# Four spectral layers on one core: tensors between layers stored by unit, image, column and row

## The chip, the cores and the metric

The kernel runs on one NeuronCore of a Trainium2 chip. The metric is the device time of one execution in microseconds (us), the median of several. The engines that are named below are TensorE (PE; its weight loads are a row of their own, PEld), VectorE (DVE), ScalarE (ACT), GpSimd (POOL), and SyncE (SP). SP computes nothing here: it issues every transfer of the kernel, on one queue, and waits in order for what each transfer needs.

## The reference

The input is `x` of shape (2, 64, 64, 384) in float32: two images, 64 rows, 64 columns, 384 channels. Four layers follow each other. Each is a two-dimensional Fourier mixer with a two-step product per block of 48 channels, and adds its input at the end:

```python
xs = jnp.fft.rfft2(xf32, axes=(1, 2)).reshape(B, H, Wm, NUM_HEADS, BLOCK)
o1r = jax.nn.relu(einsum(xr, w1[0]) - einsum(xi, w1[1]) + b1[0])   # and o1i
o2r = einsum(o1r, w2[0]) - einsum(o1i, w2[1]) + b2[0]              # and o2i
out = jnp.fft.irfft2(softshrink(o2r, LAMBDA) + 1j * softshrink(o2i, LAMBDA), s=(H, W), axes=(1, 2))
return out + x
```

Layer 1 differs: it normalises each pixel over its channels first, uses a GELU and no shrinking, keeps half of the row frequencies, and is followed by a token MLP:

```python
h = afno2d(_ln(x, ln1_g, ln1_b), w1, b1, w2, b2) + x
m = _ln(h, ln2_g, ln2_b)
return _gelu(m @ mlp_w1 + mlp_b1) @ mlp_w2 + mlp_b2 + h            # 384 -> 1536 -> 384
```

## The kernel before

The 384 channels are cut into 8 blocks of 48, and two blocks make a **unit** (96 channels, `PAIR`). So each layer has 4 units (`PAIRS`), and the four layers have 16, numbered 0 to 15; units 4 to 7 are layer 1. A unit lies in one of three SBUF buffers `xs` of 128 partitions x 64 rows x 96 channels (3072 KB): the partition is (image, column), so 64 partitions hold one image. It is loaded whole, worked on in place (the residual sum is written into it), and stored.

**The spectral part** runs over blocks `g`. POOL (in layer 1: ACT and DVE) makes `xn` from `xs`. PE then does `f1` (the transform over rows, `xn` as weights), `f2` (over columns), `m1` and `m2` (the two products), `f5` and `f6` (the inverse transforms). Except in `m1` and `f6` its matmuls are short, 32 to 96 columns, with a weight load before each. ACT and DVE move results out of PSUM between these steps; DVE's `f6` adds the last one to `xs` and so releases a quarter of the unit for its store (`res_ready`). PE's instructions of this part are written out one by one and not looped.

**The token MLP** runs over 16 tiles of 4 rows of both images, with two buffers (`r` is 0 or 1) for the tile's input `xm` and its output `om`, each 128 partitions x 4 rows x 384 channels. Its inner tiles are a loop. DVE's `statistics` of the following tile come after the fourth of twelve hidden blocks of the current one and wait for `m_loaded[r]`; its `results` wait for `m_stored[r]`.

**Transfers.** Between the layers the tensors `after[0]` to `after[3]` lie in HBM. Before, each is (image, row x column, channel), as are the input `x` and the output `out`. A partition's part of one row of a unit is then a run of 96 floats, 384 bytes. All of the order is SP's program:

- `load_rows` (L357) loads a quarter of a unit for one image, 16 rows; `load_unit` does this eight times. `store_unit` (L375) stores eight such pieces, two after each quarter is ready.
- In `units`, the load of unit n+3 stands behind the stores of unit n and waits until they have landed (`wait_stored`).
- Around the MLP: with `after[1]` complete but for unit 7, the first three units' share of tile 0 is loaded (L404); ACT copies the last unit's share from `xs`. Tile 1 is loaded (L363) in the middle of unit 7's stores. In `token_mlp_moves`, a tile is stored when DVE has finished it (L440), and the tile two further on is loaded. In the last round unit 8 is loaded but for four rows, which ACT copies from `om`. Units 9 and 10 are loaded when the last tile is stored.

The addresses of the two kinds of transfer come from these two helpers:

```python
def image(a, b, first, rows, unit):
    i = unit % PAIRS
    return a[b].rearrange("(h w) c -> w h c", w=SIDE)[:, first:first + rows, i * PAIR:(i + 1) * PAIR]

def tile_view(a, b, n):
    return a[b].rearrange("(n j w) c -> w n j c", w=SIDE, j=4)[:, bass.ds(n, 1)].rearrange("w o j c -> w (o j) c")
```

Of the kernel before, what the change touches and what calls it, by code (L numbers as in the profile page):

```python
# [7 lines left out]
F32 = mybir.dt.float32  # L8
# [3 lines left out]
BATCH, SIDE, CHANNELS = 2, 64, 384  # L12
BLOCKS, BLOCK = 8, 48
PAIR = 2 * BLOCK
PAIRS = CHANNELS // PAIR
# [4 lines left out]
TILES = BATCH * SIDE * SIDE // TOKENS  # L20
# [75 lines left out]
def groups_before(g):  # L96

    return sum(LAYER[n // BLOCKS].n for n in range(g))
# [86 lines left out]
def first_of(i):  # L185
    return isinstance(i, int) and i == 0


def wait_past(engine, semaphore, value):

    if not isinstance(value, int) or value > 0:
        engine.wait_ge(semaphore, value)


def build(nc, x, consts, spectral, lncols, ln1, cols, w1, w2, b2, out):
    with ExitStack() as ctx:
        def sb(name, shape):
            return ctx.enter_context(nc.sbuf_tensor(name, shape, F32))
# [4 lines left out]
        def sem(name):  # L203
            return ctx.enter_context(nc.semaphore(name))

        after = [nc.dram_tensor(f"after_{n}", (BATCH, SIDE * SIDE, CHANNELS), F32).ap() for n in range(4)]

        layer_in = [x, after[0], after[2], after[3]]
        layer_out = [after[0], after[1], after[3], out]
# [17 lines left out]
        with ExitStack() as scope:  # L227
# [16 lines left out]
            w = [sb(f"w{n}", [P, 2, W_ALL]) for n in range(2)]  # L244
        with ExitStack() as scope:
# [3 lines left out]
            om = sb("om", [P, 2, 4, CHANNELS])  # L249
# [10 lines left out]
            xm = sb("xm", [P, 2, 4, CHANNELS])  # L260
# [37 lines left out]
        m_loaded = [sem("m_loaded0"), sem("m_loaded1")]  # L298
        m_stored = [sem("m_stored0"), sem("m_stored1")]
# [14 lines left out]
        def image(a, b, first, rows, unit):  # L314

            i = unit % PAIRS
            return a[b].rearrange("(h w) c -> w h c", w=SIDE)[:, first:first + rows, i * PAIR:(i + 1) * PAIR]

        def residual(g, first, rows):
# [14 lines left out]
            first = g % 2 * BLOCK + k * CHAN  # L334
            return xs[buffer_of(g // 2)][:, :, first:first + CHAN].rearrange("p h c -> p c h")

        def tile_view(a, b, n):

            return a[b].rearrange("(n j w) c -> w n j c", w=SIDE, j=4)[:, bass.ds(n, 1)].rearrange("w o j c -> w (o j) c")

        block = ctx.enter_context(nc.Block())

# [2 lines left out]
        def _(sp):  # L345

            def load_weights(unit):
                layer, i = unit // PAIRS, unit % PAIRS
                if unit >= 2:
                    sp.wait_ge(w_ready, W_STEPS * (unit - 1))  # L350
                sp.dma_start(wstage[:, unit % 2, :, :],
                             spectral[layer].rearrange("(g k) p n -> p g k n", k=2)[:, i]
                             ).then_inc(w_loaded[unit % 2], 16)
# [5 lines left out]
                             ).then_inc(x_loaded[buffer_of(unit)], 16)  # L359

            def load_tile(r, n):
                for b in range(BATCH):
                    sp.dma_start(xm[b * SIDE:(b + 1) * SIDE, r], tile_view(after[1], b, n)).then_inc(m_loaded[r], 16)  # L363

            def load_unit(unit):
                for part in range(PARTS):
                    for b in range(BATCH):
                        load_rows(unit, b, part)
# [15 lines left out]
            def wait_stored(unit):  # L384
                sp.wait_ge(stored[buffer_of(unit)], LOADS * (uses_before(unit) + 1))
# [9 lines left out]
            def units(first, last):  # L395

                load_weights(first + 2)
                for unit in range(first, last):
                    if unit == 2 * PAIRS - 1:

                        for n in range(PAIRS, 2 * PAIRS - 1):
                            wait_stored(n)
                        for b in range(BATCH):
                            sp.dma_start(xm[b * SIDE:(b + 1) * SIDE, 0, :, 0:CHANNELS - PAIR],  # L404
                                         tile_view(after[1], b, 0)[:, :, 0:CHANNELS - PAIR]).then_inc(m_loaded[0], 16)
                        sp.wait_ge(f2_done, groups_before(2 * BLOCKS))
                        sp.dma_start(w2raw[:, :].rearrange("p (k n) -> p k n", k=HC),
                                     w2.rearrange("(k p) n -> p k n", p=P)).then_inc(w2_loaded, 16)
                    store_unit(unit)
                    if unit + 3 < UNITS and unit != 2 * PAIRS - 1:  # L410
                        load_weights(unit + 3)
                    if unit == 2 * PAIRS - 3:

                        wait_stored(unit)
                        sp.dma_start(w1raw[:, :].rearrange("p (k n) -> p k n", k=KC),
                                     w1.rearrange("(k p) n -> p k n", p=P)).then_inc(w1_loaded, 16)
                        sp.dma_start(b2row[:, :], b2.partition_broadcast(P)).then_inc(s_wts, 16)
                    elif unit + 3 < last:
                        wait_stored(unit)
                        if unit < PAIRS:  # L420
                            sp.wait_ge(st_done, SIDE * (unit + 1 if unit < PAIRS - 1 else STATS))
                        load_unit(unit + 3)

            def token_mlp_moves():

                wait_stored(2 * PAIRS - 1)

                def body(i, last):
                    for r in range(2):
                        if last and r == 1:  # L430

                            sp.wait_ge(m_stored[0], 16 * BATCH * TILES // 2)
                            sp.wait_ge(m_stored[1], 16 * BATCH * (TILES // 2 - 1))
                            for part in range(PARTS):
                                for b in range(BATCH):
                                    load_rows(2 * PAIRS, b, part, PART_ROWS - (4 if part == PARTS - 1 else 0))

                        sp.wait_ge(om_ready, 4 * (r + 1) + i * 8)
                        for b in range(BATCH):
                            sp.dma_start(tile_view(after[2], b, 2 * i + r), om[b * SIDE:(b + 1) * SIDE, r]  # L440
                                         ).then_inc(m_stored[r], 16)
                        if not last:
                            load_tile(r, 2 * i + (2 + r))

                iterate(sp, TILES // 2, body)
                sp.wait_ge(m_stored[1], 16 * BATCH * TILES // 2)
                sp.wait_ge(tail_copied, 1)

            sp.dma_start(const[:, 0:C_D2], consts[:, 0:C_D2]).then_inc(s_first, 16)
# [461 lines left out]
        def _(dve):  # L911
# [138 lines left out]
                    normalise(0, 0)  # L1050

            def statistics(r, i):
                dve.wait_ge(m_loaded[r], 16 * BATCH + i * (16 * BATCH))
                for j in range(4):
                    dve.bn_stats(stat[:, j, :], xm[:, r, j, :]).then_inc(st2_done, 1)
                dve.wait_ge(st2_done, 4 * (r + 1) + i * 8)
                dve.tensor_copy(counts[:, :], stat[:, :, 0])
                for j in range(4):
                    dve.bn_aggr(mv2[:, r, j, :], stat[:, j, :]).then_inc(mv2_ready, 1)
# [23 lines left out]
            def token_mlp():  # L1083
                def split_hidden(r, i, n):
                    dve.wait_ge(g_high, HC * r + n + 1 + i * (2 * HC))
                    dve.tensor_tensor(gl[:, n % 4, :], g[:, n % 2, :], gh[:, n % 4, :],  # L1086
                                      ALU.subtract).then_inc(g_low, 1)

                def results(r, i):
                    dve.wait_ge(skip_ready, r + 1 + i * 2)  # L1090
                    wait_past(dve, m_stored[r], i * (16 * BATCH))
                    for j in range(4):
                        dve.wait_ge(mm2_done, 4 * r + j + 1 + i * 8)
                        dve.tensor_tensor(om[:, r, j, :], ps[:, MM2_BANKS[j], 0:CHANNELS], xm[:, r, j, :],
                                          ALU.add).then_inc(om_ready, 1)

                def tile(r, i, following):
                    for t in range(HC):
                        if r == 0 and first_of(i):
                            split_second(t)  # L1100
                        split_hidden(r, i, t)
                        if following:
                            if t == TURN_AT - 5:
                                statistics(*following)
                            if t == TURN_AT - 3:
                                normalise(*following)
                            if 0 <= t - TURN_AT < KC:
                                split_input(*following, t - TURN_AT)
                    results(r, i)

                def body(i, last):
                    tile(0, i, (1, i))
                    tile(1, i, None if last else (0, i + 1))

                for k in range(KC):
                    split_input(0, 0, k)
                iterate(dve, TILES // 2, body)
# [219 lines left out]
```

## Time and profile before

| | us |
|---|---|
| median of 3 runs | 2069.34 |
| lowest and highest | 2063.79, 2072.46 |
| span of the profiled execution, first to last instruction | 2057.0 |
| median less that span (start and end of an execution, and the spread of runs) | 12.3 |
| PE busy in the span | 1919.2 |
| DVE, ACT, POOL busy | 1173.7, 1008.7, 435.4 |
| spectral part of layers 0 and 1 (to about 640) | 640 |
| token MLP (about 640 to 1463) | 823 |
| layers 2 and 3 (from about 1463) | 594 |

The page gives for the profiled execution its span alone; its own time is this span and what lies around it, which the page does not show. "Busy" counts the time in which an engine has an instruction in work. PE's idle time is told with what ended it: the name of another engine and instruction, or "issue", where the profile shows nothing that it waited for. A transfer is told with the time that its issue took on SP and with the time from issue to landing.

### The profile page before, as it was taken

To read this page: it belongs to the slowest core of one execution; us is meant where nothing else is said; L and a number is where in the kernel's file an instruction comes from. 1 tells how busy PE (TensorE), PEld (TensorE's weight loads), DVE (VectorE), ACT (ScalarE), POOL (GpSimd) and SP (SyncE) were. 2 spreads that over 40 slices of the span, in tenths; PEclk is the share of its full clock that TensorE was granted. 3 is DMA by queue.
4 is the path that set the end of the run, shared out by engine and by line. 5 is a ranking of instruction groups with operands and counts; after the bars stand their busy time and mean duration, and the time that the engine had idled before them with its cause. 6 is when DMAs were issued, how large, how long until landed. Compare 5 with 4: busy or idle time off the path is not lost.

```text
span 2057.0 us, 68971 instructions
## 1 busy us (share of the span) xinstructions
PE 1919.2 (93%) x31104; PEld 1570.9 (76%) x31104; DVE 1173.7 (57%) x2480; ACT 1008.7 (49%) x1644; POOL 435.4 (21%) x425
## 2 busy tenths in 40 slices
PE   4999995698998999999999999999899999999996
PEld 3777772576776999999999999999777777777774
DVE  3687887977855433333333333332377767677675
ACT  3766545576753333333333333333466666665652
POOL 3212104965631000000000000000221211221200
PEclk9999997799999999999999999999999999999998
DMA  9425738307434111111111111114532573557314
GB/s 164 100 49 85 129 62 142 55 4 129 114 86 122 32 31 31 31 31 31 31 31 31 31 31 31 31 31 73 94 53 49 87 127 80 84 99 126 60 40 96
DMA packets 299701, 141.05 MB, mean 69 GB/s; under 512 B 275760, under 2 KB 298032, under 8 KB 299440
## 3 DMA queue, kind: packets, MB, share of 16 engines
q1 hardware_dynamic: 299440, 137.08, 36.2%
q8 instruction: 224, 3.67, 0.8%
q14 instruction: 37, 0.30, 0.1%
HBM read 74.14 MB, written 62.91 MB: 67 GB/s over the span
## 4 chain that ended last, share of the span: by engine, by line
PE 80%; DVE 9%; SPq 3%; ACT 2%; issue 2%; POOL 2%; DMA 1%; DVEq 0%; POOLq 0%; ACTq 0%
PE ps L693 20%; PE ps L678 19%; PE ps L586 8%; PE ps L523 8%; PE ps L537 7%; PE ps L602 6%; PE ps L555 5%; PE ps L504 4%; DVE u L937 3%; DVE st L974 2%; SPq L357 1%; DVE xs L962 1%; PE ps L565 1%; DMA wraw<-in_w 1%; PE ps L663 1%
## 5 line engine op out<-in xcount | busy, mean ns | idle before, releaser
L1086 DVE TENSOR_TENSOR gl<-g,gh 128x512 fp32r<-128x512 f32 x192 | 156.8, 816 | 476.3 <-ACT gh L872 476.3
L937 DVE TENSOR_TENSOR u<-ps,clamp 64x192 f32<-64x192 f32 (+1 forms) x864 | 378.1, 438 | 27.7
L869 ACT ACTIVATE g<-ps,colp 128x512 f32<-128x512 f32 x192 | 132.3, 689 | 529.1 <-PE ps L678 529.1
L523 PEld LDWEIGHTS ps<-const,z 128*48 128x48 f32 x8384 | 266.0, 124 | 134.9 <-issue 128.6
L732 ACT ACTIVATE z<-ps 64x512 f32<-64x512 f32 x366 | 234.9, 642 | 155.1 <-PE ps L504 148.2
L523 PE MATMUL ps<-const,z 128*48 128x64 f32 (+1 forms) x8384 | 270.3, 217 | 10.2 <-issue 5.3
L1173 POOL COPY xn<-xs 128x512 f32<-128x512 f32 x144 | 152.0, 1096 | 535.8 <-PE ps L504 343.9
L693 PE MATMUL ps<-w2h,gh 128*128 128x384 f32 x768 | 261.9, 341 | 0.0
L693 PE MATMUL ps<-w2h,gl 128*128 128x384 f32 x768 | 258.6, 337 | 0.0
L693 PE MATMUL ps<-w2l,gh 128*128 128x384 f32 x768 | 257.5, 335 | 0.0
L586 PEld LDWEIGHTS ps<-const,u 128*64 128x64 f32 x6144 | 206.7, 139 | 52.2 <-issue 25.7
L537 PE MATMUL ps<-zf,w 112*64 112x512 f32 (+1 forms) x992 | 244.2, 566 | 1.3 <-ACT zf L758 0.9
L602 PE MATMUL ps<-v,const 128*64 128x384 f32 x1024 | 216.1, 500 | 22.5 <-DVE xs L962 20.2
L586 PE MATMUL ps<-const,u 128*64 128x64 f32 x6144 | 220.0, 225 | 15.2 <-DVE u L942 7.6
L678 PE MATMUL ps<-mth,w1h 128*128 128x512 f32 x576 | 224.9, 390 | 4.0 <-DVE mtl L1074 4.0
L775 ACT ACTIVATE h<-ps,w 113x512 f32<-113x512 f32 (+1 forms) x248 | 162.7, 656 | 133.3 <-PE ps L537 130.8
L678 PE MATMUL ps<-mth,w1l 128*128 128x512 f32 x576 | 228.0, 396 | 0.0
L678 PE MATMUL ps<-mtl,w1h 128*128 128x512 f32 x576 | 227.6, 395 | 0.0
L931 DVE TENSOR_SCALAR clamp<-ps 128x384 f32<-128x384 f32 (+1 forms) x216 | 112.6, 521 | 181.6 <-PE ps L555 180.7
L504 PEld LDWEIGHTS ps<-const,xn 64*64 64x64 f32 x6144 | 110.0, 146 | 105.7 <-issue 77.9
L504 PE MATMUL ps<-const,xn 64*64 64x64 f32 x6144 | 124.3, 234 | 61.1 <-POOL xn L1173 23.5
L555 PE MATMUL ps<-w,h 113*64 113x96 f32 x3168 | 173.7, 248 | 7.4 <-ACT h L775 5.0
(70 smaller groups left out, 2463.4 us busy)
## 6 DMA issues: line engine op xcount, KB each, us to landing
after<-xs SPq DMA_DIRECT2D x96, 384.0 KB, 5.4
xs<-after SPq DMA_DIRECT2D x94, 384.0 KB, 8.8
after<-om SPq DMA_DIRECT2D x32, 384.0 KB, 4.3
out<-xs SPq DMA_DIRECT2D x32, 384.0 KB, 5.5
xm<-after SPq DMA_DIRECT2D x30, 384.0 KB, 6.3
xs<-in_x SPq DMA_DIRECT2D x24, 384.0 KB, 8.4
wstage<-in_spectral SPq DMA_DIRECT2D x16, 210.0 KB, 5.8
xs<-in_x SPq DMA_DIRECT2D x4, 768.0 KB, 11.9
```

The costliest lines, as they stand in the source:

```text
L504: mm = pe.matmul(ps[j * SIDE:(j + 1) * SIDE, banks[b], c * SPAN:(c + 1) * SPAN], xn[rows, slot, first + j, :], const[rows, C_D1:C_D1 + SPA ...
L523: mm = pe.matmul(ps[a * SIDE:a * SIDE + BLOCK, F2_BANK, n * L.kh:(n + 1) * L.kh], z[:, g % 2, slot, :], basis(col + a * SIDE, L.kh), start ...
L537: mm = pe.matmul(ps[rows, M1_BANK, 0:width], w[unit % 2][0:MIX, g % 2, rows], zf[0:MIX, n % 2, 0:width], start=True, stop=True)
L555: mm = pe.matmul(ps[b * SIDE:(b + 1) * SIDE, bank, p * PAIR:(p + 1) * PAIR], h[0:ROWS, n % 2, c * SIDE:(c + 1) * SIDE], mix[0:ROWS, g % 2, ...
L586: mm = pe.matmul(ps[a * SIDE:(a + 1) * SIDE, bank, c * SIDE:(c + 1) * SIDE], u[:, g % 2, k * CHAN + c, BATCH * a:BATCH * a + SPAN], basis( ...
L602: mm = pe.matmul(ps[a * SIDE:(a + 1) * SIDE, F6_BANKS[row_bank(g, k)], 0:ROWCHUNK * BLOCK], basis(C_D6 + a * SIDE, SIDE), v[:, g % 2, rows ...
L678: mm = pe.matmul(ps[:, MM1_BANKS[n % 2], :], a[:, at], b[r][:, k, :], start=k == 0 and m == 0, stop=k == KC - 1 and m == 2)
L693: mm = pe.matmul(ps[:, MM2_BANKS[j], 0:CHANNELS], a[:, n % 4, part], b[:, at], start=n == 0 and m == 0, stop=n == HC - 1 and m == 2)
L732: act.activation(to, data, ACT.Copy, scale=layer_of(g).forward).then_inc(z_ready, 1)
L775: act.activation(h[0:ROWS, n % 2, 0:width], ps[0:ROWS, M1_BANK, 0:width], L.act, bias=w[g // 2 % 2][0:ROWS, g % 2, READY_BIAS:W_ALL]).then ...
L937: dve.tensor_tensor(u[to, g % 2, :, start + b:start + size:BATCH], whole, limited, ALU.subtract).then_inc(u_ready, 1)
L1086: dve.tensor_tensor(gl[:, n % 4, :], g[:, n % 2, :], gh[:, n % 4, :], ALU.subtract).then_inc(g_low, 1)
```

## The change

The four tensors between the layers get the shape (unit of the layer, image, column, row, channel of the unit). `image` and `tile_view` follow it. In `image`, a partition's 16 rows of a unit are now one run of 1536 floats, 6144 bytes, on both sides. `x` and `out` keep their layout, so the loads of units 0 to 3 and the stores of units 12 to 15 stay as they are. An MLP tile is no longer moved image by image (two transfers, 64 partitions x 4 rows x 384 channels, runs of 1536 bytes) but unit by unit: four transfers of 128 partitions x 4 rows x 96 channels. On the HBM side four rows are then one run of 1536 bytes; on the SBUF side each row is a run of 384 bytes. The counts of the MLP's semaphores follow.

```diff
-        after = [nc.dram_tensor(f"after_{n}", (BATCH, SIDE * SIDE, CHANNELS), F32).ap() for n in range(4)]
+        after = [nc.dram_tensor(f"after_{n}", (PAIRS, BATCH, SIDE, SIDE, PAIR), F32).ap() for n in range(4)]
...
             i = unit % PAIRS
+            if len(a.shape) == 5:
+                return a[i, b, :, first:first + rows, :]
             return a[b].rearrange("(h w) c -> w h c", w=SIDE)[:, first:first + rows, i * PAIR:(i + 1) * PAIR]
...
-        def tile_view(a, b, n):
+        TILE = 16 * PAIRS
-            return a[b].rearrange("(n j w) c -> w n j c", w=SIDE, j=4)[:, bass.ds(n, 1)].rearrange("w o j c -> w (o j) c")
+        def tile_view(a, i, n):
+            return a[i].rearrange("b w (n j) c -> (b w) n j c", j=4)[:, bass.ds(n, 1)].rearrange("p o j c -> p (o j) c")
+        def tile_rows(t, r, i):
+            return t[:, r, :, i * PAIR:(i + 1) * PAIR]
...
             def load_tile(r, n):
-                for b in range(BATCH):
-                    sp.dma_start(xm[b * SIDE:(b + 1) * SIDE, r], tile_view(after[1], b, n)).then_inc(m_loaded[r], 16)
+                for i in range(PAIRS):
+                    sp.dma_start(tile_rows(xm, r, i), tile_view(after[1], i, n)).then_inc(m_loaded[r], 16)
...
-                        for b in range(BATCH):
-                            sp.dma_start(xm[b * SIDE:(b + 1) * SIDE, 0, :, 0:CHANNELS - PAIR],
-                                         tile_view(after[1], b, 0)[:, :, 0:CHANNELS - PAIR]).then_inc(m_loaded[0], 16)
+                        for i in range(PAIRS - 1):
+                            sp.dma_start(tile_rows(xm, 0, i), tile_view(after[1], i, 0)).then_inc(m_loaded[0], 16)
...
-                        for b in range(BATCH):
-                            sp.dma_start(tile_view(after[2], b, 2 * i + r), om[b * SIDE:(b + 1) * SIDE, r]
+                        for n in range(PAIRS):
+                            sp.dma_start(tile_view(after[2], n, 2 * i + r), tile_rows(om, r, n)
                                          ).then_inc(m_stored[r], 16)
...
-                dve.wait_ge(m_loaded[r], 16 * BATCH + i * (16 * BATCH))
+                dve.wait_ge(m_loaded[r], TILE - (0 if r else 16) + i * TILE)
```

The engines that compute keep their instructions in the same order; only SP's change. From the last tile of the MLP to the first stores of layer 2, SP's program was this. A row gives the line, the tensors, and partitions x the rest; `x6` are six in a row.

```order
L440 DMA after<-om 64x4x384 x2
L357 DMA xs<-after 64x16x96 x6
L357 DMA xs<-after 64x12x96 x2
L440 DMA after<-om 64x4x384 x2
L357 DMA xs<-after 64x16x96 x16
L351 DMA wstage<-in_spectral 128x2x210
L375 DMA after<-xs 64x16x96 x8
```

At the same place of the changed kernel it is this.

```order
L447 DMA after<-om 128x4x96 x4
L365 DMA xs<-after 64x1536 x6
L365 DMA xs<-after 64x1152 x2
L447 DMA after<-om 128x4x96 x4
L365 DMA xs<-after 64x1536 x16
L359 DMA wstage<-in_spectral 128x2x210
L383 DMA after<-xs 64x1536 x8
```

Nothing stands elsewhere than before; each unit transfer has one run per partition in place of 16, and each tile transfer is four in place of two. At the entry of the MLP, where unit 7 is stored around the loads of tiles 0 and 1, SP's program was this.

```order
L404 DMA xm<-after 64x4x288 x2
L407 DMA w2raw<-in_w 128x12x384
L375 DMA after<-xs 64x16x96 x4
L363 DMA xm<-after 64x4x384 x2
L375 DMA after<-xs 64x16x96 x4
```

In the changed kernel it is this.

```order
L412 DMA xm<-after 128x4x96 x3
L414 DMA w2raw<-in_w 128x12x384
L383 DMA after<-xs 64x1536 x4
L371 DMA xm<-after 128x4x96 x4
L383 DMA after<-xs 64x1536 x4
```

The load of the MLP's second weights (`w2raw`) has three transfers of short runs ahead of it on SP's queue in place of two of longer ones.

## Rows read from the trace of the kernel before

**Rows 1.** The page: busy time of engines, packets by size, queue of instruction fetches.

```profile
PE 1919.2 (93%) x31104; PEld 1570.9 (76%) x31104; DVE 1173.7 (57%) x2480; ACT 1008.7 (49%) x1644; POOL 435.4 (21%) x425
...
DMA packets 299701, 141.05 MB, mean 69 GB/s; under 512 B 275760, under 2 KB 298032, under 8 KB 299440
...
q8 instruction: 224, 3.67, 0.8%
```

**Rows 2.** Stretches: length; busy PE, PEld, DVE, ACT, POOL; clock, DMA share, GB/s.

```profile
0.00:60.00 60.00, 33.80 (x856) 26.67 (x860) 22.42 (x45) 23.68 (x38) 22.41 (x36) 0.94 1.30 169
...
340.00:410.00 70.00, 37.17 (x1006) 29.08 (x1006) 59.19 (x115) 45.26 (x96) 62.91 (x56) 0.67 0.50 84
...
640.00:1460.00 820.00, 820.00 (x4199) 743.50 (x4198) 300.67 (x548) 283.75 (x429) 71.32 (x45) 1.00 0.15 34
...
1645.00:1715.00 70.00, 68.75 (x1684) 51.79 (x1680) 49.13 (x105) 43.52 (x72) 14.17 (x18) 1.00 0.55 96
```

**Rows 3.** SP's waits: line, whom it waited for: total us, times, longest.

```profile
SPq L375 <- DVE xs L962: 792.9, 60, 91.9
SPq L440 <- DVE om L1094: 684.7, 15, 46.9
```

**Rows 4.** Timelines (start, us, what, idle before): a unit load's issues; its user.

```profile
1603.54 14.13 SPq L357 DMA_DIRECT2D xs<-after  x8
...
1623.95 4.28 POOL L1173 COPY xn<-xs 128x512 f32<-128x512 f32 x4 [14.08 <-DMA xs<-after]
```

**Rows 5.** PE's waits that ended in "issue", whole span: total us, times, longest.

```profile
PE ps L504 <- issue: 17.5, 12, 3.4
...
PE ps L523 <- issue: 5.3, 6, 1.5
```

**Rows 6.** PE's timeline inside loads of units 4, 7 (middle four rows) and 15.

```profile
243.59 0.24 PE L555 MATMUL ps<-w,h 113*64 113x96 f32 x1 [0.90 <-issue]
...
497.12 0.67 PE L504 MATMUL ps<-const,xn 64*64 64x64 f32 x26
500.42 1.34 PE L504 MATMUL ps<-const,xn 64*64 64x64 f32 x38 [2.63 <-issue]
...
509.64 0.92 PE L504 MATMUL ps<-const,xn 64*64 64x64 f32 x45
513.07 0.56 PE L504 MATMUL ps<-const,xn 64*64 64x64 f32 x19 [2.51 <-issue]
...
1902.63 0.21 PE L504 MATMUL ps<-const,xn 64*64 64x64 f32 x1 [1.43 <-issue]
```

**Rows 7.** The page's DMA issues: count, KB each, median us from issue to landing.

```profile
xs<-after SPq DMA_DIRECT2D x94, 384.0 KB, 8.8
...
w1raw<-in_w SPq DMA_DIRECT2D x1, 2304.0 KB, 9.4
```

**Rows 8.** PE's timeline while `w1raw` is loaded (issued at 558.23).

```profile
565.64 0.46 PE L504 MATMUL ps<-const,xn 64*64 64x64 f32 x15 [2.23 <-issue]
```

**Rows 9.** The stretch of the MLP in which unit 8 is loaded (columns of rows 2).

```profile
1418.00:1440.00 22.00, 22.00 (x112) 19.94 (x111) 4.15 (x6) 7.00 (x11) 0.00 (x0) 1.00 0.86 134
```

**Rows 10.** Timelines of DVE, ACT, SP, POOL and PE around the waits on loads.

```profile
512.86 1.06 DVE L994 TENSOR_TENSOR xn<-xs,mv 128x512 f32<-128x512 f32 x1 [4.90 <-DMA xs<-after]
...
625.45 2.59 ACT L886 ACTIVATE w2h<-w2raw 128x384 fp32r<-128x384 f32 x6 [1.23 <-DMA w2raw<-in_w]
633.38 1.49 ACT L860 ACTIVATE mt<-ps,colp 128x512 f32<-128x512 f32 x2 [5.34 <-PE ps L663]
...
1468.60 30.65 SPq L357 DMA_DIRECT2D xs<-after  x16
...
1489.33 4.19 POOL L1173 COPY xn<-xs 128x512 f32<-128x512 f32 x4 [13.36 <-DMA xs<-after]
...
1495.63 0.91 PE L504 MATMUL ps<-const,xn 64*64 64x64 f32 x44
```

More of the change, by code:

```diff
@@ L430, in body @@
                         if last and r == 1:
-                            sp.wait_ge(m_stored[0], 16 * BATCH * TILES // 2)
-                            sp.wait_ge(m_stored[1], 16 * BATCH * (TILES // 2 - 1))
+                            sp.wait_ge(m_stored[0], TILE * TILES // 2)
+                            sp.wait_ge(m_stored[1], TILE * (TILES // 2 - 1))
                             for part in range(PARTS):
@@ L445, in token_mlp_moves @@
                 iterate(sp, TILES // 2, body)
-                sp.wait_ge(m_stored[1], 16 * BATCH * TILES // 2)
+                sp.wait_ge(m_stored[1], TILE * TILES // 2)
                 sp.wait_ge(tail_copied, 1)
@@ L1090, in results @@
                     dve.wait_ge(skip_ready, r + 1 + i * 2)
-                    wait_past(dve, m_stored[r], i * (16 * BATCH))
+                    wait_past(dve, m_stored[r], i * TILE)
                     for j in range(4):
```

## The prediction, made before the changed kernel was run

> **What bounds the kernel now.** I read the busy times first. PE is busy for 1919.2 of 2057.0 us [rows 1], the next engine, DVE, for 1173.7. A change of transfers can therefore only win from PE's 137.8 idle us, or lose by making new ones. The stretches say where they are [rows 2]: 26.2 us of idle lie in the first 60 us, where the kernel waits for `x`, whose layout stays; none in the 820 us of the MLP; 1.25 us in 70 in a typical unit of layers 2 and 3, although the DMA engines are busy for over half of it. Next I asked whether SP, the queue that the change rewrites, is late anywhere. It waits 792.9 us for DVE's residual sums before the stores and 684.7 us for DVE's MLP results [rows 3]. So stores are paced by the computation, and a faster store wins nothing by itself. Loads of units start when the third unit before them is stored: one is issued from 1603.54 on, and POOL goes on with it at 1623.95 [rows 4]. That is 20.4 us for 3072 KB, and POOL waited 14.08 us for it, but PE did not: there is no PE wait for POOL's `xn` in that stretch, because the ring `xn` is ahead.
>
> That leaves one link between transfers and PE, the idle time that the profile calls "issue". It ends 17.5 us of waits ahead of L504 and 5.3 ahead of L523, the two largest such rows [rows 5]. The pauses fall in the middle of a group of matmuls that waits once, at its start: 26 matmuls of `f1`, then 2.63 us of nothing, then the other 38; again after 45, then 2.51 us [rows 6]. A semaphore cannot explain a stop in the middle; late instructions can. The page has a queue of instruction fetches with 224 packets in 3.67 MB, 16.4 KB each [rows 1]. And they fall where units are loaded: of PE's pauses of this kind of 0.6 us or more, 14 lie inside or just at the end of a load of units 4 to 15. In order of time they are 0.90, 1.03, 1.08, 1.45, 2.63, 2.51, 0.95, 0.72, 1.35, 1.47, 1.25, 0.82, 0.84 and 1.43 us; rows 6 show the first, the fifth and sixth, and the last. Their sum is 18.4 us. I read this as: while the DMA engines work off the load, the next block of PE's instructions comes late. That it is a fetch is my inference from where the pauses fall.
>
> **The change part by part.**
>
> *Unit loads and stores in long runs.* In 192 transfers (96 stores, 96 loads) 1024 pieces of 384 bytes become 64 of 6144. 96 x 1024 stores and 96 x 1024 loads (two of the loads are a quarter shorter) are about 195,000 of the 275,760 packets under 512 bytes [rows 1]. The nearest row for the new kind is the load of `w1raw`, whose runs are 6144 bytes too: 2304 KB in 9.4 us [rows 7]. At its rate a unit takes 3072/2304 x 9.4 = 12.5 us instead of 20.4, a factor of 0.61; a single piece of a load takes 8.8 us now from issue to landing [rows 7], with others in between. The other bound is no gain, 20.4 us, if SP or a 64-partition transfer sets the pace.
>
> What is it worth? By itself nothing, since PE waits for no unit. DVE waits 4.90 us for unit 7 [rows 10], but that wait lies over PE's own pause of 2.51 us, and PE waits for no DVE result behind it: 0, at best 4.9. The value is in the pauses. Their number should fall with the length of a load (0.61), as fewer fetches meet one. The length of a pause should fall too, if a fetch waits for the transfer whose turn it is: each of the eight pieces of a load took 20.4/8 = 2.55 us and would take 12.5/8 = 1.57, again 0.61. The pause of 1.45 us lies at the start of layer 1, where POOL is busy for 62.91 of 70 us and PE for 37.17 [rows 2], so POOL's chain would take it up; I count 18.4 - 1.4 = 17.0 us on the path. What stays is 17.0 x 0.61 x 0.61 = 6.4 us, so the gain is 10.6 us. The bounds: all of it goes (-17.0), or long runs hold up the fetches more (the rival below, +14).
>
> *MLP tiles in short runs.* A tile's load and its store are 512 pieces of 1536 bytes before and 2048 pieces of 384 bytes after. A unit load moves 8192 such pieces in 20.4 us, so a tile's load takes about 5.1 us and its store as much. SP waits up to 46.9 us for each tile [rows 3], and the load is wanted a tile later: hidden. Would 384-byte pieces disturb PE in the MLP as they do elsewhere? The trace shows it: unit 8 is loaded in such pieces inside the MLP, with the DMA engines busy at 0.86, and PE is busy for 22.00 of 22.00 us [rows 9]. Its matmuls are long there (4199 in 820 us [rows 2]), so it needs few instructions. Cost 0.
>
> *SP's queue at the MLP's ends.* Ahead of `w2raw` stand three transfers with 1536 short pieces, some 3.8 us by the rate above, in place of 512 longer ones; it may land some 2 us later. ACT waited 1.23 us for it, split half of it in 2.59 us and then idled 5.34 us until PE's transposes [rows 10]: the 5.34 us cover it, cost 0. With the cover gone it would cost the excess over 5.3. At the other end, the loads of units 9 and 10 wait for the last tile's store, perhaps 3 us longer in short pieces. They started at 1468.60, POOL had unit 9 at 1489.33, PE wanted its `xn` at 1495.63 [rows 10]. Now it would be there at about 1471.6 + 12.5 = 1484. Cost 0.
>
> *Weighed against the Trainium skill.* The row first: two pauses of over 2.5 us stand in the middle of `f1` groups [rows 6]. "Runtime: NRT & Kernel Launch", section "Instruction fetch mechanics", says that blocks of 16 KiB are fetched ahead in sequence and that this is hidden, since the sequencer dispatches more slowly than the blocks arrive. By it there is nothing to win and the sum would be 0; the block size agrees with 16.4 KB per packet [rows 1], the hiding does not agree with the pauses. "DMA: Bandwidth & Descriptors", section "Queues, rings and completion order", says that a DMA engine takes turns between its queues packet by packet. It would let a fetch wait for data ahead of it, as I assume.
>
> The sum is -10.6 us: a span of 2046.4 in place of 2057.0, and for the median 2069.3 - 10.6 = 2058.7 us.
>
> **The rivals.**
>
> *Long runs hold the fetches up (slower).* The one pause during a load in 6144-byte runs is as bad as those in short ones: 2.23 us while `w1raw` came in for 9.4 us [rows 7, 8], 0.24 us per us of load. Loads of 11 units outside the MLP at 12.5 us each are 137.5 us; at that rate PE loses 32.6 us in place of 18.4: +14.2 us, 2083.5. It decides from 18.4/137.5 = 0.134 us per us upwards. Against it: the same stretch, layer 1, is where PE's matmuls are shortest, and the short runs of unit 7 cost 2.63 + 2.51 us in some 21 us there [rows 6], also 0.24.
>
> *The pauses depend only on how long a load lasts.* This is that last comparison taken seriously: equal rates for short and long runs. Then 17.0 x 0.61 = 10.4 us stay, the gain is 6.6 us: 2062.7.
>
> *Nearly all pauses go.* If a fetch has a margin and only the longest waits exceed it, waits of at most 1.57 us leave almost nothing: -15 to -17 us, 2052 to 2054.
>
> *No link (the page's hiding, or a load that is no faster).* If the pauses have another cause, or a 64-partition transfer is as slow as now, the time stays at 2069.3, give or take what the runs differ by.
>
> **How the numbers follow.** Forecast (gain of 8 to 14 us): 0.40. All pauses gone: 0.14. Pauses by length of load (gain of 3 to 8): 0.17. No link (within 3 us): 0.13. Slower by long runs (5 to 15 us or more): 0.16. The likeliest is the forecast, 2058.7. A measurement of this kernel can tell about 0.5%, 10.3 us, from no change; faster by more than that is below 2059.0. Some 0.29 of the forecast's 0.40 falls there, with all of the 0.14: 0.43. Slower by more than 0.5% is the upper part of the last case, 0.12. The rest, 0.45, is within. For 8 in 10 the range goes from 2050, just below "all gone", to 2078, which takes in the lower half of the slower case.
>
> **What the changed profile would show.** A unit load from first issue to POOL's copy in about 12 to 14 us, and SP's issue of its eight transfers in some 4 us in place of 14.13; some 145,000 packets under 512 bytes and not 275,760 (195,000 go, the MLP's tiles bring 65,000); the "issue" rows of L504, L523, L586 and L555 down by 8 to 14 us together; PE still without idle time in the MLP, with a DMA share there of 0.2 to 0.3; the 4.90 us wait of DVE gone. I would be wrong if pauses in the middle of groups are as long or longer in loads that last 12 us, if a load still takes 20 us, or if PE shows waits at the MLP's two ends that it didn't have.

## The result, and the profile after

The changed kernel is slower: 2080.47 us (median of 6 runs, 2078.02 to 2091.05) against 2065.67 us (6 runs, 2054.05 to 2072.46), a ratio of 1.008 with a 95% interval of 1.0053 to 1.0106. The forecast was 2058.7 us and its range ended at 2078. Two executions of later runs, at 2535 and 3158 us with a granted clock of 0.72 and 0.65 against 0.97 to 0.98 in all others, are left out of every median and ratio.

The page of the changed kernel first: span, busy time, packets by size, instruction fetches. It answers to [rows 1].

```profile
span 2080.2 us, 69130 instructions
...
PE 1932.8 (93%) x31104; PEld 1577.8 (76%) x31104; DVE 1173.5 (56%) x2480; ACT 1009.4 (49%) x1644; POOL 433.5 (21%) x425
...
DMA packets 165541, 141.06 MB, mean 68 GB/s; under 512 B 145696, under 2 KB 151584, under 8 KB 165280
...
q8 instruction: 224, 3.67, 0.8%
```

The packets are as forecast (145,696 under 512 bytes). The same work took 23.2 us more of span. PE is busy 13.6 us longer with the same 31104 matmuls and idle 9.6 us longer. Its waits that end in "issue" are these (line, us in total, times, longest), to be held against [rows 5]:

```profile
PE ps L530 <- issue: 17.5, 7, 3.6
...
PE ps L511 <- issue: 12.3, 8, 3.7
...
PE ps L562 <- issue: 5.4, 3, 2.6
PE ps L593 <- issue: 4.2, 3, 2.8
...
PE ps L609 <- issue: 1.6, 2, 1.0
```

They sum to 41.0 us. Before, with the rows of L586 (3.0), L555 (1.5) and L565 (0.4) added to [rows 5], they were 27.7. There are no more pauses than before (23 against 24) but longer ones. Of the 18.4 us of pauses that the prediction counted none exceeded 2.63 us; now a load of layers 2 and 3 costs PE 2 to 3.6 us at one go. The timeline of PE in the loads of units 11, 13 and 15 (start, us, what, the idle time before):

```profile
1629.16 0.26 PE L530 MATMUL ps<-const,z 128*48 128x64 f32 x1 [2.83 <-issue]
...
1766.94 0.94 PE L530 MATMUL ps<-const,z 128*48 128x64 f32 x26
1771.45 0.55 PE L530 MATMUL ps<-const,z 128*48 128x64 f32 x5 [3.56 <-issue]
...
1771.90 1.49 PE L609 MATMUL ps<-v,const 128*64 128x384 f32 x3
...
1920.48 0.39 PE L593 MATMUL ps<-const,u 128*64 128x64 f32 x7 [2.79 <-issue]
```

The 1.49 us for three matmuls of L609 are a second loss; in the kernel before three of the same line (L602 there) take 0.81 us. The granted clock is at its lower level there, for 3.4 us from about the end of the pause. The stretches around this pause and one of 320 us (columns of [rows 2]: after the length PE, PEld, DVE, ACT, POOL; then clock, DMA share, GB/s):

```profile
1767.00:1771.00 4.00, 0.88 (x28) 0.73 (x24) 1.11 (x4) 0.69 (x1) 0.00 (x0) 1.00 1.03 227
1771.00:1773.00 2.00, 1.55 (x11) 1.15 (x13) 0.00 (x0) 0.60 (x1) 0.00 (x0) 0.53 0.69 154
1773.00:1776.00 3.00, 3.00 (x54) 2.75 (x52) 0.97 (x2) 0.60 (x1) 1.57 (x2) 0.75 0.04 12
1776.00:1780.00 4.00, 4.00 (x136) 3.20 (x134) 2.65 (x6) 2.15 (x4) 1.42 (x2) 1.00 0.02 4
...
1640.00:1960.00 320.00, 308.54 (x7370) 231.53 (x7366) 216.52 (x464) 192.11 (x314) 63.27 (x76) 0.98 0.39 88
```

0.53 and 0.75 are mostly 1.2 GHz in place of 2.4. The trace has four such intervals of 3.4 us between 1640 and 1960; before there is none. In that stretch PE did 7678 matmuls before and was busy for 315.10 us; after it did 7370 in 308.54. Of the 4% that are missing, some 12.8 us of 320, 6.6 are idle time, and four intervals of 3.4 us at half speed explain up to 6.8.

What happened to the transfers is in the timelines of SP and POOL (as [rows 4]):

```profile
1612.35 4.97 SPq L365 DMA_DIRECT2D xs<-after  x8
...
1757.34 5.38 SPq L365 DMA_DIRECT2D xs<-after  x8
...
1774.43 2.13 POOL L1180 COPY xn<-xs 128x512 f32<-128x512 f32 x2 [8.81 <-DMA xs<-after]
```

All loads of units together (the row of their line):

```profile
DMA to landing us min/median/max: 4.3/8.7/22.5
```

A load is there 17.1 us after its first issue (1757.34 to 1774.43; the other four of layers 2 and 3 took 16.4 to 18.2). Before it took 20.4 us, and the forecast was 12.5, so the gain is less than forecast. The issues are what changed most: SP put all eight transfers on the queue in 5 us in place of 14.13. Before, the longest of these transfers landed 10.3 us after its issue; now one needs up to 13.8 us when one unit is loaded, and 22.5 us where units 9 and 10 are issued together. Both are signs of a longer backlog. It can be worked out from the trace, as the bytes of the transfers that SP has issued (each counted evenly over its issue) less the bytes of the packets that have ended: in the loads of units 11 to 15 it reached 836 to 956 KB before and 2121 to 2339 KB after. The DMA engines themselves were not busier. Their share (the sum of the packets' times, which can pass 1) was 1.06 to 1.08 in these loads before and 0.84 to 0.85 after, so how busy they are does not explain the longer pauses.

The MLP and its ends kept their cost of nothing. A tile's stores and loads take 2.1 and 2.4 us of issue, its rounds are 51.4 us apart as before, and `w2raw` landed within 10.5 us (10.9 before). PE is busy for all of 650 to 1455 us in both kernels.

### The profile page after: what moved, and what is told of

It reads as the page before. It is cut to its first block, busy times and chain, and to the rows that moved or that the text cites. A ratio compares the mean times of both kernels' runs of the same rounds, so it can differ in the third digit from the quotient of the medians.

```text
span 2080.2 us, 69130 instructions
## 1 busy us (share of the span) xinstructions
PE 1932.8 (93%) x31104; PEld 1577.8 (76%) x31104; DVE 1173.5 (56%) x2480; ACT 1009.4 (49%) x1644; POOL 433.5 (21%) x425
## 2 busy tenths in 40 slices
DMA packets 165541, 141.06 MB, mean 68 GB/s; under 512 B 145696, under 2 KB 151584, under 8 KB 165280
## 4 chain that ended last, share of the span: by engine, by line
PE 80%; DVE 9%; SPq 3%; issue 3%; ACT 2%; POOL 2%; DMA 1%; DVEq 0%; POOLq 0%; ACTq 0%
PE ps L700 19%; PE ps L685 19%; PE ps L530 8%; PE ps L593 8%; PE ps L544 7%; PE ps L609 7%; PE ps L562 5%; PE ps L511 4%; DVE u L944 3%; DVE st L981 2%; SPq L365 1%; DVE xs L969 1%; PE ps L572 1%; DMA wraw<-in_w 1%; PE ps L670 1%
## 5 line engine op out<-in xcount | busy, mean ns | idle before, releaser
L944 DVE TENSOR_TENSOR u<-ps,clamp 64x192 f32<-64x192 f32 (+1 forms) x864 | 377.7, 437 | 27.7
L609 PE MATMUL ps<-v,const 128*64 128x384 f32 x1024 | 220.2, 509 | 24.1 <-DVE xs L969 20.1
L969 DVE TENSOR_TENSOR xs<-ps,xs 128x384 f32<-128x384 f32 x256 | 141.7, 555 | 72.8 <-PE ps L609 67.7
```

The costliest lines, as they stand in the source:

```text
L609: mm = pe.matmul(ps[a * SIDE:(a + 1) * SIDE, F6_BANKS[row_bank(g, k)], 0:ROWCHUNK * BLOCK], basis(C_D6 + a * SIDE, SIDE), v[:, g % 2, rows ...
L944: dve.tensor_tensor(u[to, g % 2, :, start + b:start + size:BATCH], whole, limited, ALU.subtract).then_inc(u_ready, 1)
L969: dve.tensor_tensor(to, ps[:, F6_BANKS[row_bank(g, k)], 0:ROWCHUNK * BLOCK].rearrange("p (h c) -> p h c", c=BLOCK), to, ALU.add).then_inc( ...
```

## The experiments

The two theories. **Backlog** (A): PE's instructions are fetched by the same DMA engines; a fetch waits for what is queued ahead of it, and how much that is depends on how fast SP issues. Rivals: **something else of the change** (B: the short MLP tiles, the layout, the long stores), or **long pieces as such** (A2). All runs are held against runs of the kernel before on the same chip; medians of different runs can come from different chips, so it is the ratios that compare them. A profile shows one execution of a kernel. The recorded expectations number the runs in the order in which they were made: first, 384-byte loads; second, pair by pair (the paced run); third, the same in the kernel before; fourth, 1536 bytes; fifth, halves; sixth, pairs but not unit 7; seventh, more transfers paced; eighth, one transfer at a time; ninth, the same in the kernel before; tenth, `w1raw` with it.

Each kernel's sum of issue waits holds 4.8 us that do not change with the transfers: a pause of 1.44 us (1.45 before) at the start of layer 1 and one of 3.4 us at the entry of layer 2, of the same length in all twelve kernels.

### Back to 384-byte pieces, in the loads alone

```diff
+                if unit >= PAIRS and unit != 2 * PAIRS:
+                    at = part // 2 * 2 * PART_ROWS
+                    to, data = (t.rearrange("w (g two j) c -> w two g (j c)", two=2, j=1)[:, part % 2]
+                                for t in (xs[...][b * SIDE:(b + 1) * SIDE, at:at + 2 * PART_ROWS, :],
+                                          image(layer_in[unit // PAIRS], b, at, 2 * PART_ROWS, unit)))
```

The cut `xs[...]` stands for the unit's buffer. A transfer takes every other row of 32, so that no two of its rows join. Unit 8, which is loaded inside the MLP, keeps its long pieces.

> The changed kernel, but a unit load reads every other row of 32 rows, so that its pieces are 384 bytes again; layout, stores (6144 bytes) and MLP tiles stay as changed. Theory A (long pieces make a backlog on the DMA engines that the instruction fetches wait behind): PE's waits that end in issue fall from 41.0 us to 25 to 31, a load takes 19 to 21 us, the median falls to 2063 to 2070. Rival B (the loss is in the short MLP tiles, the new HBM layout or the long stores): the median stays at 2077 to 2083 and the pauses stay above 38 us.

Measured: 2059.95 us, ratio 0.9987 (0.9971 to 1.0004). Issue waits of 31.0 us, SP's issues of a load:

```profile
1603.70 14.22 SPq L372 DMA_DIRECT2D xs<-after  x8
```

The whole loss is gone, with the new layout, the long stores and the short MLP tiles still in place. That takes out B: those three together cost nothing that can be measured, and win nothing either.

### 1536-byte pieces

The same edit with `j=4`, so that a piece is four rows.

> As the first run, with pieces of 1536 bytes. Theory A: between the two, since the backlog that SP can build is between: issue waits of 28 to 38 us, a load of 14 to 18 us, median 2066 to 2077. A rival with a best length (pieces long enough to be efficient, short enough to be paced by their issue): issue waits below 24 us, median under 2062.

Measured: 2081.97 us, ratio 1.0104 (1.0068 to 1.014), as slow as with 6144 bytes. I had expected the middle. The waits of its two largest lines, and then the issues of unit 11's load in SP's timeline:

```profile
PE ps L535 <- issue: 15.8, 7, 3.3
PE ps L516 <- issue: 12.4, 8, 3.4
```

```profile
1612.89 6.66 SPq L372 DMA_DIRECT2D xs<-after  x8
```

All issue waits sum to 39.5 us, a little over the 38 expected, and the backlog reached 1971 to 2209 KB. So the length of a piece is not the measure. What this run shares with the changed kernel, and not with the one before, is that eight transfers are issued in 5 to 7 us. With pieces of 384 bytes SP takes 14 us for eight transfers, and the backlog stayed at 920 to 1027 KB in the first run.

### Long pieces, but pair by pair

```diff
                 for part in range(PARTS):
+                    if part and unit >= PAIRS:
+                        sp.wait_ge(x_loaded[buffer_of(unit)], LOADS * uses_before(unit) + 16 * BATCH * part)
                     for b in range(BATCH):
```

> The changed kernel, with SP waiting before each pair of a unit's load transfers until the pair before it has landed, so that never more than 768 KB of a load is outstanding; pieces stay 6144 bytes. Theory A1 (what counts is the backlog of bytes ahead of a fetch): no pause of PE over 1.5 us in a paced load, issue waits below 22 us, a load of 18 to 24 us that PE doesn't wait for, median 2052 to 2062. Rival A2 (a fetch suffers from long pieces as such, however few are queued): issue waits stay above 33 us, median 2073 or more.

Measured: 2057.38 us (median of nine), ratio 0.9977 (0.9959 to 0.9995), in the range of A1; A2 is out. The issue waits are 24.1 us, a little over the 22 expected, and the longest pause in a paced load is 2.51 us (unit 7) where A1 had none over 1.5. The unit that layer 1 is short of, 7, came later, and PE's timeline shows one reason why the gain isn't larger: 4.7 us of PE's wait for DVE at L611 stand behind DVE's wait for the load.

```profile
PE ps L513 <- issue: 13.7, 9, 3.4
PE ps L532 <- issue: 5.9, 5, 1.5
...
DVE xn L1003 <- DMA xs<-after: 11.8, 1, 11.8
```

### The same pacing in the kernel before

The same two lines in `load_unit` of the kernel before.

> The kernel before (384-byte pieces in loads and stores) with the same pacing of the unit loads. Theory A1: its own pauses (27.7 us of issue waits) fall too, to 12 to 20 us, median 2054 to 2062; a load takes 22 to 28 us. Rival A2 (only long pieces hold fetches up, short ones pause PE for another reason): no change, 2063 to 2069.

Measured: 2069.78 us (median of nine), ratio 1.0036 (1.0019 to 1.0053): slower, which neither side had. The pauses did not fall (issue waits 28.5 us), and PE waited for the late unit 7:

```profile
526.30 1.55 PE L604 MATMUL ps<-v,const 128*64 128x384 f32 x4 [7.14 <-DVE xs L964]
```

SP's issue already paces 384-byte pieces; a wait per pair made a load longer (unit 11's from 1617.66 to POOL's copy at 1644.60, 26.9 us in place of 20.4) and took no pauses away, though the backlog in the loads of units 11 to 15 fell to 734 to 752 KB. Theory A does not explain this. The run left open whether a smaller backlog would help the kernel before at all; the ninth run is on that.

### Half a load at a time, and one transfer at a time

The wait of the paced run at `part == 2` alone leaves up to 1536 KB queued. The other ends of the scale leave unit 7 unpaced (`unit != 2 * PAIRS - 1`), with pairs, or with a wait before each transfer:

```diff
                     for b in range(BATCH):
+                        if part + b and unit >= PAIRS and unit != 2 * PAIRS - 1:
+                            sp.wait_ge(x_loaded[buffer_of(unit)],
+                                       LOADS * uses_before(unit) + 16 * (BATCH * part + b))
                         load_rows(unit, b, part)
```

> The changed kernel, with one wait in the middle of a unit load: up to 1536 KB outstanding, in place of 3072 (changed kernel) and 768 (the paced run). Theory A1 (a fetch waits for the bytes that are queued ahead of it): between the two, issue waits of 28 to 38 us, median 2062 to 2074. Rival A3 (any gap in the load lets the fetch through): as the paced run, 24 us, 2056 to 2060.

> As the paced run, but unit 7, for which DVE waited 11.8 us there and PE's L611 4.7 us behind it, is loaded unpaced. If that wait was on the path, the gain over the paced run is the 4.7 us of PE less the unit's longer pauses (3.7 + 2.5 in place of 5.5 us): 2 to 5 us, median 2053 to 2057. If PE's wait was taken up elsewhere: the same as the paced run within 1 us.

> As the sixth, but each of the eight transfers of a load waits for the one before: 384 KB outstanding. Theory A1: pauses smaller again, issue waits of 15 to 21 us; a load takes 28 to 34 us, and where PE doesn't wait for it (units 11 to 15) nothing is lost, median 2048 to 2056. Rival A4 (a load that lasts longer meets more fetches, each delayed by about as much): issue waits as in the sixth or more, 2055 to 2062.

Measured, in order of what the program lets stand in the queue. The backlog is the most that the trace shows in the loads of units 11 to 15, worked out as above, and the last column is PE's waits that end in issue between 1520 and 1990 us, where these units are loaded:

| pieces, queued at most | backlog KB | median us | ratio to before (95%) | issue waits, whole span | issue waits, 1520 to 1990 |
|---|---|---|---|---|---|
| long, 3072 KB (changed kernel) | 2121 to 2339 | 2080.47 | 1.008 (1.0053 to 1.0106) | 41.0 | 14.6 |
| 1536 bytes, 3072 KB | 1971 to 2209 | 2081.97 | 1.0104 (1.0068 to 1.014) | 39.5 | 13.2 |
| long, 1536 KB | 1356 to 1392 | 2073.82 | 1.0055 (1.0036 to 1.0075) | 35.3 | 9.8 |
| 384 bytes, 3072 KB (first run) | 920 to 1027 | 2059.95 | 0.9987 (0.9971 to 1.0004) | 31.0 | 9.0 |
| 384 bytes, 3072 KB (before) | 836 to 956 | 2065.67 | 1 | 27.7 | 6.3 |
| long, 768 KB | 744 to 751 | 2057.38 | 0.9977 (0.9959 to 0.9995) | 24.1 | 4.2 |
| long, 768 KB, not unit 7 | 742 to 749 | 2052.42 | 0.995 (0.9931 to 0.9969) | 23.0 | 1.9 |
| 384 bytes, 768 KB (third run) | 734 to 752 | 2069.78 | 1.0036 (1.0019 to 1.0053) | 28.5 | 7.8 |
| long, 384 KB, not unit 7 | 361 to 369 | 2049.49 | 0.9935 (0.9913 to 0.9957) | 17.8 | none |

The waits fall with the backlog, in every row but that of the third run. Between two executions of like pacing they can differ by 2 us (4.2 and 1.9), so the 9.0 and 6.3 of the two kernels with 384-byte loads are not far apart. With one transfer at a time a load takes twice as long, and PE has no idle time at all in 320 us. SP's timeline and the stretch:

```profile
1603.04 31.07 SPq L365 DMA_DIRECT2D xs<-after  x8
```

```profile
1640.00:1960.00 320.00, 320.00 (x7848) 240.28 (x7845) 230.33 (x494) 204.08 (x335) 68.95 (x83) 1.00 0.40 95
```

These are 7848 matmuls against 7678 before and 7370 after, in the same 320 us. Rival A4, that a longer load meets more delays, fell with it, and A3, that any gap in a load lets a fetch through, with the halves. The run with pairs and unit 7 unpaced was 5 to 6 us faster than the run with unit 7 paced (medians 2052.42 and 2057.38 on two chips; their ratios to before, 0.995 and 0.9977, say 0.27% or 5.6 us, with intervals that overlap a little). This speaks for DVE's wait having been on the path; it is a little more than the 2 to 5 us expected, and the median lies just under the 2053 us.

The trace has a record of each packet, and those of 16 KB are the fetches. The longest time between two of them around each load of units 11 to 15, in us:

| kernel | units 11 to 15 |
|---|---|
| before | 7.5, 7.0, 7.3, 6.9, 7.2 |
| changed | 8.9, 8.8, 11.4, 9.0, 10.2 |
| changed, 384-byte loads | 6.3, 6.6, 8.2, 6.7, 8.6 |
| changed, 768 KB queued | 7.4, 6.1, 6.0, 6.2, 6.3 |

PE's pause at 1767.9 to 1771.45 of the changed kernel lies around a fetch that the record shows at 1768.6, 11.4 us after the one before it; between the loads of units 11 and 12 they follow each other in 3.7 to 5.9 us. This measure is rough: a record does not say whose instructions it brings, the 384-byte loads reach 8.6 us without the loss, and spacings with 384 KB queued reach 7.8 us with no pause.

Two other readings of the same records tie the pauses to fetches. Counted from 70 us on, the twelve kernels have 140 pauses of 0.6 us or more that end in issue, beside the two in each that are the same everywhere. All 140 fall at the same place, within one instruction, in steps of 256 of PE's recorded instructions (one place ahead of the MLP, another behind it), as they would if PE ran out at the end of a block. And each ends 1.2 to 1.8 us after one of the 16 KB packets has ended. So the pauses are late fetches, by position and by time. What a fetch waits for, from when it is asked for, no record shows; that the backlog sets it is read from the doses above.

### More transfers paced

Unit 3's load from `x` and `w1raw` (three transfers in place of one).

> As the sixth, and the load of unit 3 is paced too and w1raw comes in three transfers of 768 KB, each after the other has landed. Theory A1: the pauses at 175 to 186 us (1.2 and 0.65 us) and the one of 1.5 to 2.2 us beside w1raw shrink to under 1 us each: 2 to 3 us less than the sixth, median 2050 to 2055. Rival: those pauses have another cause: no change.

Measured: 2054.12 us, ratio 0.9954 (0.9936 to 0.9972): no different from the sixth. The pause beside `w1raw` went (1.47 us in the sixth run), with its runs as long as ever and only fewer of them queued, but the two in unit 3's load stayed, at 1.56 and 1.74 us (1.22 and 0.65 in the sixth). That load is in 384-byte pieces, which pacing by pairs did not help in the kernel before either.

### One transfer at a time in the kernel before, and with `w1raw`

> The kernel before (384-byte pieces everywhere) with each transfer of a unit load but unit 7's waiting for the one before it. Theory A1: the backlog is as short as in the eighth run, so its issue waits fall from 27.7 to 16 to 22 us and the median to 2048 to 2058, within 5 us of the eighth run; the layout then matters by its shorter transfers alone. Rival C (384-byte pieces hold fetches up in their own way, as the third run's 2070.7 us suggests): 2062 or more.

Measured: 2066.32 us, ratio 1.0002 (0.9985 to 1.002), neither the 2048 to 2058 of A1 nor C's reason. PE's waits (the same columns), and from its timeline the wait for unit 11:

```profile
PE ps L507 <- POOL xn L1176: 37.8, 9, 18.2
...
PE ps L507 <- issue: 13.3, 7, 3.4
...
PE ps L526 <- issue: 1.2, 1, 1.2
PE ps L589 <- issue: 1.0, 2, 0.6
```

```profile
1639.98 1.16 PE L507 MATMUL ps<-const,xn 64*64 64x64 f32 x64 [2.09 <-POOL xn L1176]
```

The pauses did fall as theory A says, to 15.8 us with the 0.3 of a smaller line, and between 1520 and 1990 us there is none, at a backlog of 365 to 378 KB. What took their place is POOL's `xn`: PE waited 37.8 us for it in place of 23.5, because eight short-piece transfers one by one take 32 to 35 us to issue and the unit lands after PE wants it: PE waits 0.8 to 3.4 us for each of units 11 to 15 and 5.2 us for unit 9. So the shorter backlog pays only with the long pieces: the same scheme with them takes 31 us, and of these waits only one of 2.9 us for unit 9 is left. With pacing, and only then, the changed layout is worth something (0.9935 against 1.0002, with intervals apart).

> The eighth run, with w1raw also in six transfers of 384 KB, one after another. Theory A1: the pause of 2.03 us beside w1raw goes; 1 to 2 us less than the eighth run (0.9935 of before), 0.992 to 0.994. Rival: DVE's split of w1 waits for it and loses as much: 0.994 to 0.996.

Measured: 2048.5 us, ratio 0.992 (0.9894 to 0.9946), within the expected span but not to be told from the eighth run's 0.9935 by its interval. The pause beside `w1raw` is gone; DVE waited 5.3 us for it instead, and PE 4.2 us for DVE behind that, so the profile bears out the rival and gives this step no gain. By its median it is the fastest kernel of this study: the changed kernel with the pacing above and six transfers for `w1raw`, 0.8% faster than before and 1.6% faster than as changed.

## Why the prediction was wrong

**What bounds the kernel** was read rightly, down to the one link between transfers and PE. The pauses called "issue" were the right rows, and that transfers lengthen them is now shown by experiment and not by their place alone. One of the fourteen was not of this kind: the 1.45 us at the start of layer 1 is there in every kernel, whatever is loaded. The sum left it out all the same, for another reason.

**The term that failed** is the length of a pause, and with it the sign. I let a fetch wait for one transfer's share, 2.55 us before and 1.57 after, and so multiplied by 0.61 a second time. Counted as the prediction counted them, and without the one at the start of layer 1, 13 pauses of 17.0 us became 13 of 30.9: a mean of 1.31 us became 2.38, a factor of 1.8 in place of 0.61. In layers 2 and 3 alone 8 pauses of 8.8 us became 8 of 20.5. What fits the doses is that a fetch waits for what is queued ahead of it. The number for that stood in the rows: 14.13 us of SP's time for eight issues [rows 4]. I read it as time that SP could spare, from the rows on SP's waits [rows 3], and wrote of a shorter issue only as a thing that would show in the profile. In fact SP was held up by the short pieces, and that kept the queue short. The 1536-byte run shows it at its plainest: pieces a quarter as long as the changed kernel's, nearly the same fast issue, the same loss.

**The rival that came true** is the first, long runs holding up the fetches, by its time (2083.5 forecast, 2080.47 measured), though not by its reason. That its time came so close is partly luck: it put 32.6 us of pauses into 137.5 us of loads at a fixed rate, while the 30.9 us measured fell into loads that took 16 to 18 us each and not 12.5, and the clock added to them. Its evidence was the single pause of 2.23 us beside `w1raw` [rows 7, 8], whose 2304 KB are queued at once: a backlog, and not a matter of 6144-byte runs, as the seventh run shows, where the same runs in three parts left no such pause. I held against it that unit 7's short pieces cost as much per us of load. That was so, and in layer 1 it changed least (2.63 and 2.51 us became 3.71 and 2.49). The comparison that I needed was with the pauses of layers 2 and 3, where short pieces cost 0.7 to 1.5 us at a time. It had a chance of 0.16, too little for a case that had a row of its own for it.

**The time of a load** was forecast at 12.5 us from `w1raw` and measured at 16.4 to 18.2. That is 0.8 to 0.9 of before in place of 0.61. PE waits for no unit, so the term bore on the count of pauses only, and the count did not fall at all: 13 and 13. The first factor of 0.61 failed too.

**A cost that had no term** is the clock. The prediction took a pause for its own length. In four of the five loads between 1600 and 1960 a pause of 2.00 to 3.56 us was followed by 3.4 us at 1.2 GHz (the fifth, of 2.83 us, was not); this explains up to 6.8 of the 12.8 us lost between 1640 and 1960. Before, all pauses between 1600 and 1960 were under 1.5 us, and the clock stayed at 2.4 GHz.

**What held:** the stores, the MLP tiles in short runs, and the queue at the MLP's ends cost nothing (the first experiment); PE was full in the stretch 1418 to 1440 of [rows 9], and is again under the changed load. Few fetches are due there: 11 between 665 and 1455 us in both kernels, against 89 (before) and 87 (changed) in the 470 us from 1520 to 1990. The DMA share of the MLP was 0.13 (0.15 before), below the 0.2 to 0.3 that I had forecast. The 4.90 us wait of DVE for unit 7 went, and bought nothing, since a pause of 3.71 us took its place. The Trainium skill, "Runtime: NRT & Kernel Launch", section "Instruction fetch mechanics", says that instruction fetch is hidden. The runs do not agree: the issue waits go from 17.8 to 41.0 us with the backlog. The Trainium skill, "DMA: Bandwidth & Descriptors", section "Queues, rings and completion order", says that a DMA engine goes round its queues packet by packet. Taken alone, that would let a fetch pass a long backlog after one packet of it. The runs do not agree with that either: the waits grew with what was queued, from none between 1520 and 1990 us at 384 KB to 14.6 us at 3072 KB.

**The base:** I took 12.3 us between span and median for start and end. The runs list 2082.01 us for a span of 2080.2, so it is 1.8 us; the rest was the spread of runs. The profiled execution of before was shorter than its median, and of the 23.2 us between the spans about 15 (14.8 between the medians) are the change.

## What to carry to other kernels

A transfer that no engine waits for can still cost time: PE's own instructions come over the same DMA engines, and the straight-line code of short matmuls needed a block every 5 us here where the looped MLP needed 11 in 790 us. Before a transfer is made more efficient, ask what its slowness was pacing. If its issue becomes fast, put a wait between its parts, so that little is queued at once; where there is slack, the slowest load that still arrived in time was the best one here (31 us in place of 17), and where there was none (unit 7) it was better left unpaced.

## What the runs showed of the hardware that I had not expected

- SP's time for eight transfers of 384 KB (loads of one unit outside the MLP) was 13.0 to 14.4 us with 1024 pieces each, but 5.2 to 6.7 us with 256 pieces and 4.9 to 5.9 with 64. So from 1536 bytes per piece on, longer pieces issued little faster.
- Longer pieces made a load little faster: 20.4 us with 384 bytes, 16.4 to 18.2 with 6144.
- With nothing queued but one transfer of 384 KB, all pauses of PE in layers 2 and 3 vanished but for the 3.4 us at their entry, while the same bytes were moved in the same stretch.
- All pauses of PE of 0.6 us or more that changed with the transfers fell at the same place in steps of 256 of its instructions, and ended 1.2 to 1.8 us after a packet of the fetch queue.
- Left open: why 384-byte pieces paced by pairs kept their pauses (28.5 us of issue waits, 734 to 752 KB of backlog), and whether the length of the queue counts in bytes or in time. No run separates these.
